# Gated delta attention on one core: the slot table of the delta stage laid out anew

## The reference

```
q = silu(conv4(h @ Wq)); k = silu(conv4(h @ Wk)); v = silu(conv4(h @ Wv))
q = l2norm(q) * scale; k = l2norm(k)
beta = sigmoid(h @ Wb); g = -exp(A_log) * softplus(h @ Wa + dt_bias)
for each t:
    S = S * exp(g_t)
    delta = (v_t - k_t S) * beta_t
    S = S + k_t (x) delta
    o_t = q_t S
x = x + (rmsnorm(o) * silu(h @ Wg)) @ Wo
```

## Time and profile before

| | |
|---|---|
| time, median of 3 runs (lowest to highest) | 3790.98 us (3790.16 to 3799.99) |
| the profiled execution: time, span | 3798.17 us, 3795.2 us |
| busy in the span: TensorE, VectorE, ScalarE, GpSimd | 87%, 72%, 54%, 48% |
| mean granted clock of TensorE | 0.951 |
| the first projection tile's taps on VectorE start, the last's | 77.2 us, 1561.1 us |

### The profile page before, as it was taken

One profiled execution on the slowest core, in us unless ns is written; L12 is line 12 of the kernel. 1 busy time (PEld: TensorE's weight loads), 2 busy tenths in 40 slices (PEclk: granted clock), 3 DMA queues, 4 the chain that ended last, 5 costly groups with the idle time before them and its releaser, 6 DMA issues. The chain is left out here.

```text
span 3795.2 us, 87218 instructions
## 1 busy us (share of the span) xinstructions
PE 3294.0 (87%) x32714; PEld 2466.9 (65%) x32714; DVE 2723.1 (72%) x5753; ACT 2038.1 (54%) x4599; POOL 1804.8 (48%) x1647
## 2 busy tenths in 40 slices
PE   4789999999999999968999999986898599899998
PEld 3577777777777777745666566654666366656665
DVE  5577777777777777647777677775999477767775
ACT  3456565656565656513666366632444366636662
POOL 3355555555555555434666166632122466526662
PEclk8689999999999999989999999997999799999999
DMA  4111111111111111033122321222112222131122
GB/s 123 23 24 25 25 25 25 26 25 26 24 27 24 27 25 24 11 95 81 43 53 56 93 50 44 71 79 55 47 50 55 63 49 64 45 95 44 46 71 70
DMA packets 409630, 182.71 MB, mean 48 GB/s; under 512 B 235808, under 2 KB 384384, under 8 KB 406656
## 3 DMA queue, kind: packets, MB, share of 16 engines
q1 hardware_dynamic: 409216, 177.15, 19.0%
HBM read 94.47 MB, written 40.12 MB: 35 GB/s over the span
## 5 line engine op out<-in xcount | busy, mean ns | idle before, releaser
L1197 POOL TENSOR_TENSOR delta_cv<-delta_cv,delta_last_tap 96x256 f32<-96x256 f32 (+1 forms) x384 | 332.7, 867 | 623.4 <-DVE delta_cv L1631 623.4
L1938 POOL TENSOR_TENSOR g_a_rn<-g_a_clip,g_minus_half 128x16 f32<-128x16 f32 x64 | 186.4, 2912 | 271.2 <-DVE g_a_clip L2202 243.0
L1938 POOL TENSOR_TENSOR f_a_rn<-f_a_clip,f_minus_half 128x16 f32<-128x16 f32 x64 | 186.3, 2911 | 260.7 <-DVE f_a_clip L2202 232.5
L2155 ACT ACTIVATE g_a_pr<-g_ps,g_a_nb,g_a_rn 128x128 f32<-128x128 f32 x512 | 185.5, 468 | 146.4 <-DVE g_a_nb L2236 146.4
L2155 ACT ACTIVATE f_a_pr<-f_ps,f_a_nb,f_a_rn 128x128 f32<-128x128 f32 x512 | 185.5, 468 | 146.4 <-DVE f_a_nb L2236 146.4
L1466 ACT ACTIVATE delta_cv<-delta_ps,delta_conv_qk 96x256 f32<-96x256 f32 x256 | 120.9, 472 | 253.5 <-PE delta_ps L1299 252.7
L1623 DVE SCALAR_TENSOR_TENSOR delta_cv<-delta_ps,delta_conv_qk,delta_cv 96x256 f32<-96x256 f32 x256 | 122.1, 477 | 169.5 <-ACT delta_last_tap L1468 169.2
L1243 PE MATMUL delta_ps<-delta_state,delta_qk 96*128 96x192 f32 x1024 | 199.4, 339 | 27.3 <-issue 22.8
L1623 DVE SCALAR_TENSOR_TENSOR delta_cv<-delta_ps,delta_conv_v,delta_cv 128x256 f32<-128x256 f32 x192 | 92.1, 480 | 155.5 <-ACT delta_last_tap L1468 154.1
L1243 PEld LDWEIGHTS delta_ps<-delta_state,delta_qk 96*128 96x128 f32 x1024 | 168.3, 193 | 41.7 <-issue 38.1
L1466 ACT ACTIVATE delta_cv<-delta_ps,delta_conv_v 128x256 f32<-128x256 f32 x192 | 90.5, 471 | 127.5 <-PE delta_ps L1299 127.5
(11 more groups left out here) (350 smaller groups left out, 10477.3 us busy)
## 6 DMA issues: line engine op xcount, KB each, us to landing
f_a_vm<-f_a_v SPq DMA_DIRECT2D x128, 130.0 KB, 2.3
g_a_vm<-g_a_v SPq DMA_DIRECT2D x128, 130.0 KB, 2.3
delta_gd<-delta_dram_row SPq DMA_DIRECT2D x16, 1024.0 KB, 4.6
window_vm<-window_v SPq DMA_DIRECT2D x64, 128.0 KB, 2.3
f_m_x<-y SPq DMA_DIRECT2D x24, 256.0 KB, 3.5
delta_dram_inv<-delta_sub SPq DMA_DIRECT2D x16, 256.0 KB, 2.1
f_m_more<-x SPq DMA_DIRECT2D x16, 256.0 KB, 3.9
x<-f_m_x SPq DMA_DIRECT2D x16, 256.0 KB, 2.3
```

What stands on the lines that cost most here:

```text
L1197: pool.tensor_tensor(cv[0:M, t % 3], cv[0:M, t % 3], last_tap[0:M, t % 3], ALU.add).then_inc(summed.sem, 1)
L1938: pool.tensor_tensor(rn[:, u % 2], clip[:, u % 2], minus_half[:], ALU.pow).then_inc(rn_sb.sem, 1)
L2155: e = act.activation(pr[:, u % 2, half, i, :], ps[:, score_bank(u, half), i * P:(i + 1) * P], ACT.Exp, bias=nb[:, u % 2, half, i:i + 1], s ...
```

## The change

It moves steps of the delta stage to other slots, and keeps their number, but for two:

- the output's projection `y` of a chunk is cut into three parts of four products, each in its own bank, slots 25, 26, 27 of the chunk in place of 27. The first part is added to the residual, the others to the sum so far: three additions for one.
- GpSimd's power of the norms is one instruction on 128x16 in place of two on 128x8.

Moved are: the gate products (no two in one slot); the scans (heads 0 to 3 four slots ahead of the unit, heads 4 to 7 to slots 8 and 9); the second k·q product, vt, y6 of the second chunk; the 32x32 transpositions, a slot behind y4; the output's sum of squares and its power; q_eps; the rates of the diagonal blocks, a slot earlier; on the queue the decays' load, the betas' load and the load of ht.

```
@@ -986,23 +986,35 @@
 
     K_NORM = 15
     SOLVE_AT = 16
-    KK_AT, KQ_AT = ((6, 7), (9, 10)), ((13, 14), (17, 18))
-    INVERT_AT = dict(x4=23, y4=25, x5=28, y5=30, x6=32, y6=34)
-    GATE_AT, OT_AT, Y_AT = (2, 2, 5), (21, 22, 25), 27
+    SCAN_AT = ((-4, -3), (8, 9))
+    KK_AT, KQ_AT = ((6, 7), (9, 10)), ((13, 14), (18, 20))
+    VT_AT = ((20, 21), (23, 24), (26, 28), (29, 30))
+    INVERT_AT = dict(x4=(23, 24), y4=(25, 26), x5=(28, 29), y5=(30, 31), x6=(32, 33), y6=(34, 36))
+    TURN_AT = (26, 27)
+    GATE_AT, OT_AT, Y_AT = ((6, 10, 11), (2, 7, 11)), (19, 22, 23), (25, 26, 27)
+
+    def scanned(t, cc, i):
+
+        when = SCAN_AT[i][cc]
+        if when < 0 and t < SLOTS + when:
+            return 0 if t == cc else None
+        return unit(t, when)
 
     def misc_uses(t):
 
-        for k, when in enumerate(GATE_AT):
-            C = chunk(t, when)
-            if C is not None:
-                yield "gate", C, k
...
@@ -1100,13 +1112,13 @@
             load_ht(1)
             sp.wait_ge(zeroed, ZEROED)
             for t in range(LAST):
-                n = unit(t, 31)
+                n = unit(t, START + HALF + GATE_AT[1][2] - SLOTS + 1)
                 if n is not None and n + 2 < UNITS:
                     take(sp, ("gate", 2 * n - 1, 2))
                     load_ht(n + 2)
                 C = chunk(t, 4)
                 if C is not None:
-                    copied(sp, ("y", C - 2))
+                    copied(sp, ("y", C - 2, 2))
                     sp.dma_start(yres[:, C % 2], yd[C * P:(C + 1) * P, :]).then_inc(y_in[C % 2].sem, 16)
                 n = unit(t, KQ_AT[1][1] + 1)
                 if n is not None and n + 1 < UNITS:
@@ -1125,12 +1137,12 @@
                     sub_sb.need(sp, n - 1)
                     inv_out.need(sp, n - 1)
                     sp.dma_start(sub[:, 0], diag_d.rearrange("b c h j i -> (b c h) j i")).then_inc(diag_in.sem, 16)
+                    betas = row_d[1, 2 * H * n:2 * H * (n + 1), :].rearrange("r (b i) -> b r i", i=16)
+                    sp.dma_start(sub_beta[:], betas).then_inc(beta_in.sem, 16)
                     brk_sb.need(sp, n - 1)
                     for b in range(B16):
                         squares = diag_d[b].rearrange("c h j i -> (j i) (c h)")[0:256:17, :]
                         sp.dma_start(n2k[16 * b:16 * b + 16, :], squares, allow_slow_non_contiguous=True).then_inc(n2k_in.sem, 16)
-                    betas = row_d[1, 2 * H * n:2 * H * (n + 1), :].rearrange("r (b i) -> b r i", i=16)
-                    sp.dma_start(sub_beta[:], betas).then_inc(beta_in.sem, 16)
                 n = unit(t, SOLVE_AT + 4)
                 if n is not None:
                     sub_sb.need(sp, n)
@@ -1147,9 +1159,9 @@
                                 r = slice(16 * b, 16 * b + 16)
                                 sp.dma_start(u16[r, :, :, 16 * (b % 4):16 * (b % 4) + 16], inv_d[0, b].rearrange("c h k i -> k c h i"))\
                                     .then_inc(u16_in.sem, 16)
-                C = chunk(t, Y_AT + 1)
+                C = chunk(t, Y_AT[2] + 1)
                 if C is not None:
-                    copied(sp, ("y", C))
+                    copied(sp, ("y", C, 2))
                     row = C // PER * ROWS + PAD + C % PER * P
...
@@ -1200,18 +1212,18 @@
                 if n is not None:
                     n2k_sb.need(pool, n)
                     bvr_sb.need(pool, n - 2)
-                for cc in range(2):
-                    n = unit(t, K_NORM + cc)
-                    if n is not None:
-                        ins = pool.tensor_tensor(rn[:, n % 2, cols(cc)], n2[:, n % 2, cols(cc)], minus_half[:, 0:H], ALU.pow)
-                        if cc == 1:
-                            ins.then_inc(rn_sb.sem, 1)
-                n = unit(t, K_NORM + 6)
+                    pool.tensor_tensor(rn[:, n % 2], n2[:, n % 2], minus_half[:], ALU.pow).then_inc(rn_sb.sem, 1)
+                n = unit(t, K_NORM + 7)
                 if n is not None:
                     rates_sb.need(pool, n)
                     copied(pool, ("x4", n - 1, 1))
                     pool.tensor_tensor(bm[:], nbrk[:, n % 2].unsqueeze(2).to_broadcast([P, 2 * H, 32]),
                                        merge[:].unsqueeze(1).to_broadcast([P, 2 * H, 32]), ALU.mult).then_inc(bm_sb.sem, 1)
+                C = chunk(t, 14)
+                if C is not None:
+                    ostat_step.need(pool, C)
+                    o_normed.need(pool, C - 1)
+                    pool.tensor_tensor(of[:], ostat[:, 1, :], minus_half[:, 0:H], ALU.pow).then_inc(of_sb.sem, 1)
                 for i in range(2):
                     C = chunk(t, 14 + i)
                     if C is not None:
@@ -1219,11 +1231,6 @@
                         copied(pool, ("gate", C, 2))
                         mine = o[:, C % 2, HB * i:HB * i + HB, :].rearrange("p h v -> p (h v)")
                         pool.tensor_tensor(mine, mine, gate[:, HB * i * DV:HB * (i + 1) * DV], ALU.mult).then_inc(o_gated.sem, 1)
-                C = chunk(t, 12)
-                if C is not None:
-                    ostat_step.need(pool, C)
-                    o_normed.need(pool, C - 1)
-                    pool.tensor_tensor(of[:], ostat[:, 1, :], minus_half[:, 0:H], ALU.pow).then_inc(of_sb.sem, 1)
                 for i in range(2):
                     C = chunk(t, 16 + i)
...
                         filled(mm, ("ot", C, k))
-                C = chunk(t, Y_AT)
-                if C is not None:
-                    copied(pe, ("ot", C, 2))
-                    bank = claim(pe, ("y", C))
-                    for m in range(NV):
-                        mm = pe.matmul(ps[:, bank, 0:D], ot[:, m, :], wo[:, m, :], start=m == 0, stop=m == NV - 1)
-                    filled(mm, ("y", C))
+                for k, when in enumerate(Y_AT):
+                    C = chunk(t, when)
+                    if C is not None:
+                        copied(pe, ("ot", C, k))
+                        bank = claim(pe, ("y", C, k))
+                        for m in range(4 * k, 4 * k + 4):
+                            mm = pe.matmul(ps[:, bank, 0:D], ot[:, m, :], wo[:, m, :], start=m == 4 * k, stop=m == 4 * k + 3)
+                        filled(mm, ("y", C, k))
                 for i in range(2):
                     for cc in range(2):
...
                             .then_inc(q_summed.sem, 1)
-                C = chunk(t, 3)
+                C = chunk(t, 6)
                 if C is not None:
                     q_summed.need(dve, C)
...
             def misc(t):
-                C = chunk(t, Y_AT)
-                if C is not None:
-                    y_in[C % 2].need(dve, C // 2)
-                    stored[C % 2].need(dve, C // 2 - 1)
-                    bank = take(dve, ("y", C))
-                    emptied(dve.tensor_tensor(out[:, C % 2], ps[:, bank, 0:D], yres[:, C % 2], ALU.add), ("y", C))
+                for k, when in enumerate(Y_AT):
+                    C = chunk(t, when)
+                    if C is not None:
+                        if k == 0:
+                            y_in[C % 2].need(dve, C // 2)
+                            stored[C % 2].need(dve, C // 2 - 1)
+                        else:
+                            copied(dve, ("y", C, k - 1))
+                        bank = take(dve, ("y", C, k))
+                        emptied(dve.tensor_tensor(out[:, C % 2], ps[:, bank, 0:D], (yres if k == 0 else out)[:, C % 2], ALU.add),
+                                ("y", C, k))
                 for cc in range(2):
                     for i in range(2):
                         mine = slice(HB * i, HB * i + HB)
...
             def diagonal_rates(t):
-                n = unit(t, SOLVE_AT)
+                n = unit(t, SOLVE_AT - 1)
                 if n is not None:
                     diag_in.need(dve, n)
                     beta_in.need(dve, n)
@@ -1701,13 +1715,13 @@
 
...
@@ -1716,6 +1730,8 @@
                         e = dve.tensor_tensor(left, t16[q, cc], ps[q, bank, 0:H * 32].rearrange("p (h b s) -> p h b s", h=H, b=2),
                                               ALU.add)
                     emptied(e, ("y4", n, cc))
+                n = unit(t, TURN_AT[cc])
+                if n is not None:
```

85 lines of the change are left out of this document (46 added, 39 removed).

## The result

The changed kernel takes 3836.9 us (median of 4 runs, 3828.8 to 3841.4) against 3795.5 for the kernel before in the same series (3790.2 to 3802.9). The ratio is 1.0107, 95% interval 1.0087 to 1.0127: slower by 1.1%, where 3719 was forecast. The profiled execution took 3828.8 us, its span 3827.0. Of the 31.8 us between the two spans, 31.5 have been lost when the next stage starts its first product on TensorE (1686.59 us, before 1655.10): 1.5 us before the first unit's K, 24.0 in the 15 steps from unit to unit, and 6.0 behind the last K.

A forecast was written before the change was run, and what follows sets the result against it. TensorE was taken to bound the delta stage, busy 84.9 of 93.86 us a unit. Gains of 1.91 + 1.69 + 0.44 + 0.75 = 4.79 us a unit, 72 us over 15 steps, gave 3719 us against the median; range 3675 to 3772.

The forecast's parts named there:

- From K to y4: From VectorE emptying the last k·k product (K, slot 10) to TensorE's y4 (slot 25): 45.95 to 44.04 us, decays ending last.
- rival 1: Slot 24: the decays land before VectorE arrives and do not end last; 2.6 us a unit more gained, 3680 us; chance 0.14.
- The scans come to slots 8 and 9 ... I take nothing: VectorE ahead of K: 2.42 us of scans come, 1.74 us of q_eps go from slot 9; cost taken as nothing.
- Rival 2: Slots 8 and 9: both scans wait for GpSimd's output multiplies; 1.7 us a unit lost, 3744 us; chance 0.12.
- y4 to K: From y4 to the next unit's K, TensorE's own work: 47.9 us in the prediction, forecast to become 45.0 us.
- Gates, transposes and vt, moved to other slots, are the same instructions: Between y4 and the next K: moving these steps to other slots was taken to leave their cost unchanged.
- the output's projection in three parts ... I cost them at nothing: Slots 4, 5, 18, 19: four more VectorE additions a unit, taken as covered; up to 1.6 us a unit without cover.
- The scans out of slots 0 to 3 and the transposes, 2.13 us: Between y4 and K: TensorE's delta_x waits go, 1.69 us, and one group of four transposes moves before y4, 0.44 us.
- I let it go: 2.25 us gained ... one short half-clock stretch: TensorE's clock: the long stretch after slots 1 and 2 goes, 2.25 us; a short one behind slot 25 costs 1.5; net 0.75.
- Rival 5: Slot 25: one gathered TensorE wait keeps the clock at half; loss above 14 us of it a unit; 3829 us; chance 0.08.
- The rule weighed in the prediction: Slots 8 and 9: VectorE instructions with two SBUF inputs and GpSimd's SBUF reads exclude each other; scans could wait, giving 3744 us.

The follow-up runs named there:

- run 14: Run 9 with only the scans of heads 4 to 7 put back from slots 2 and 3 to slots 8 and 9: 3747.7 us.
- run 9: Changed kernel, scans of heads 4 to 7 in slots 2, 3, their k·q in 17, 18, projection parts in slots 4, 5, 7 and 18, 19, 21: 3714.5 us.
- run 12: Kernel before with only the output's projection cut into three parts, in slots 3 to 5 and 17 to 19: 3845.5 us.
- run 6: Run 4 with the output's projection back in one part, in slots 5 and 19: 3731.4 us.
- run 4: Changed kernel with the scans of heads 4 to 7 in slots 2 and 3 and their k·q product back in slots 17 and 18: 3769.0 us.
- run 15: Run 9 with only the k·q product of heads 4 to 7 in slots 18 and 20, as in the changed kernel: 3788.9 us.
- run 2: Changed kernel with only the k·q product of heads 4 to 7 back in slots 17 and 18: 3806.0 us.
- run 3: Kernel before with only the scans moved, those of heads 4 to 7 to slots 8 and 9: 3797.9 us.
- run 5: Run 4 with one vt transposition group moved from slot 0 to slot 27: 3763.7 us.
- run 13: Run 9 with the second chunk's first gate product moved from slot 22 to slot 27: 3720.8 us.

## Why the prediction was wrong

**"From K to y4", 44.04 us: right in its chain, short by 1.3.** The fused power (16.08 to the solve's start for 16.26) and the solve (11.30 for 11.23) are right. The decays do end last: rival 1 is out. Mis-sized is the stretch from the solve's end, 17.9 for 16.55 us: over 11 units the queue reaches the decays' transfer after 11.2 us, where I took 10.33 from one unit, and the landing takes 5.0 us in the mean (7.1 at most), where I took 4.6.

**"The scans come to slots 8 and 9 ... I take nothing": this step failed first.** It cost 33 us alone and 47 in the changed kernel (40 by the ratios). I set the scans' 2.42 us against 1.74 us of `q_eps`, and these were themselves a wait for GpSimd that stays in the slot. Rival 2 had the mechanism and named the place, but priced it at 1.7 us a unit, taking half of it as slack, and put it against gains elsewhere. It has both scans waiting; only the one in slot 9 does. In place of slack, slot 9 ends at K, where a chain begins that is 45 us long and has no reserve; little absorbs a delay there (run 14 against run 9: y4 to K 2.7 us longer, K to y4 0.3 shorter).

**"Gates, transposes and vt, moved to other slots, are the same instructions" and "the output's projection in three parts ... I cost them at nothing": this step failed next.** I counted additions on VectorE and asked whether they are covered, but each part is also a claim of a shared bank. A third claim in a slot waits for an emptying in the same slot, by an engine that can be behind. In the kernel before, the three parts alone lose 55 us (run 12); without the third uses in slots 3 and 17 they gain (run 9 against run 6, 17 us). The change put the late k·q into slots 18 and 20, and so had kept slot 17 at two uses, but not slot 3. So the 55 us of runs 4 and 12 are not its price here: slot 3 is 1.4 us longer with the third use (4.95 against 3.54 us, the changed kernel against run 14), some 20 us in all, and the one run that undid it in the changed kernel gained 8.

**The scans out of slots 0 to 3 and the transposes, 2.13 us: this term came to 0.5 us.** The waits on `delta_x` in x5 and y5 went, but waits for `ot` and the gate came in their place, in slots with three uses. Before, y4 to K is 48.1 us with 5.6 of them at half clock, so 45.6 us without, at 0.44 us each. In run 9, with none at half clock, it is 45.2. That this is near the 45.0 us that I had forecast is luck: those held 1.5 us of a short half-clock stretch that run 9 does not have.

**"I let it go: 2.25 us gained ... one short half-clock stretch": nearly right in y4 to K.** There the changed kernel has 4.0 us at half clock, where I expected one stretch of 3.4 (before 5.6). But that one stretch was to be all of a unit, and the part from K to y4 has 4.3 us more of it (before 3.4), so that the unit has about what it had. Rival 5 priced a microsecond rightly and asked for 14 of them before the change turns into a loss; it is not that rival. What the forecast did not price is that the new wait is paid twice: run 15 lost 2.9 us by the wait for the decays and 2.9 by the clock behind it.

The parts fit together for y4 to K, forecast at 45.0 us and measured at 50.8 (runs 9, 14 and 2 have no half clock in this part):

- run 9, with none of the suspects: 45.2 us;
- the scans back in slots 8 and 9 (run 14): 47.9, so 2.7 more;
- the third use in slot 3 besides (run 2): 49.1, so 1.2 more, where the slot itself grew by 1.4;
- the late k·q besides (the changed kernel): 50.8, so 1.7 more, which is the 4.0 us at half clock at 0.44 each.

Of the 5.8 us too many, the scans are 2.7, the third use in slot 3 is 1.2, the term of 2.13 us fell short by 1.7, and the clock by 0.2. With 1.3 us in K to y4, a unit of the middle takes 7.1 us more than forecast. Outside the middle, the stretch behind the last K grew by 6.0 us, where I had taken it as unchanged; no run tells why.

That run 3 costs so little has two reasons in its trace. In slot 9 the scan's 2.8 us replace the 1.74 us of `q_eps`, 1.1 us more. And its half clock in y4 to K falls from 5.6 to 1.9 us a unit, which gives 1.6 us back; why it falls, no run tells.

The rule weighed in the prediction (the Trainium skill, SBUF — State Buffer, section "SBUF: two separate sides") was right in kind, and I should have followed it: of VectorE's scan and GpSimd's instructions only one ran at a time. By that rule the second waits for the first; in this trace a scan let three instructions in a row pass.

## What to carry to other kernels

Where two buffers are shared in turn by all side steps, count the claims in each step of the schedule before the instructions: a third claim ties the engine that bounds the kernel to whichever engine empties the bank in that slot, and splitting or moving a step is then no free edit. What it costs depends on the slot: in slots 3 and 17 together 55 us (run 9 against run 4), in slot 0 no more than the noise (run 5). And look twice at an instruction that takes ten times as long as elsewhere: `q_eps`, 1.74 us for 0.16, was a wait, and when it was moved away the scan took the wait over. A delay is priced by the place where it falls: ahead of a chain without reserve it counts in full, and a stall of TensorE of up to 4 us cost its length once more in clock (run 15). Undo the suspects one by one on a good kernel and not only on the changed one: the late k·q is worth 31 us on the changed kernel and 74 on run 9.

## What the runs showed of the hardware

A VectorE scan with two SBUF inputs that starts while GpSimd works waits for a whole row of GpSimd instructions, if there is no gap between them, and not for one only: 1.21 us became 3.73 us behind a multiply, a tap sum and a multiply (64 scans: 1209 ns at least, 1226 in the median, 3739 at most), 2.8 us behind two (run 3) and 2.17 us behind one (run 13). In each of these three it ended 1.1 us after the last GpSimd instruction. The other way round a tap sum that starts 0.16 us into a scan takes 1.60 us for 0.73.

The tiny `q_eps` (128x8) takes 0.16 us, and 1.74 us where it starts while GpSimd's tap sum and multiply run in a row (before, slot 9).

The granted clock of TensorE stayed at 1.00 over a whole unit where its longest wait was 1.3 us (run 9), and was 0.50 for 13.6 us in a unit with a wait of 4.15 us, from 2.0 us after the wait's start on (run 15). Eight microseconds a unit at half clock is what this stage had before and after the change, and the order of steps alone avoids nearly all of it.
